# Gather issue, placement order and job pacing in a one-core graph layer

## The reference, cut to what matters

```
h = relu(layernorm(x))
feat = [h[src], h[dst]]                       # 8448 x 2048
e_f = relu(feat @ W_kind + b_kind)            # kind hh: edges 0..127, oo: next 640, ho: the rest
logit = e_f @ W_a + b_a
alpha = softmax of logit over the edges of one dst
z = segment_sum(alpha * h[src], dst)
h_new, o_new = relu([h, z] @ W_hn + b) on nodes 0..63, relu([h, z] @ W_on + b) on the other 192
x = x + [h_new, o_new]
h = relu(layernorm(x)); Wd = zeros.at[src, dst].add(edge_weight)
out = x + h @ Wd.T + bias
```

## Time and profile before

| | us |
|---|---|
| median of 3 runs (lowest, highest) | 346.76 (345.24, 348.99) |
| time of the profiled execution | 346.23 |
| its span on the core | 344.4 |

### The profile page before, as it was taken

How to read it: one execution, slowest core, us unless ns; L and a number is a source line. 1 busy time by engine, 2 the same in 40 slices (tenths; PEclk the granted TensorE clock), 3 DMA queues, 4 the chain that set the end, 5 groups by cost and what they waited for, 6 DMA issues and landing times.

```text
span 344.4 us, 4123 instructions
## 1 busy us (share of the span) xinstructions
PE 308.0 (89%) x1354; PEld 194.6 (57%) x1359; DVE 253.5 (74%) x428; ACT 177.0 (51%) x435; POOL 156.1 (45%) x148
## 2 busy tenths in 40 slices
PE   0899799999768999989999999999999786998992
PEld 0687488745425665556557576666653635543531
DVE  4655427369930699969969969978999799994334
ACT  3963342373441366654846657663638466564111
POOL 3210057237740277776757757774777610000000
PEclk9999899999989999999999999999999987899997
DMA  7999969969999789999999999999999999997003
GB/s 270 337 362 414 367 254 395 387 233 335 416 409 409 281 305 410 413 409 407 418 408 409 410 410 413 411 410 412 407 411 410 409 409 407 409 408 267 2 0 122
DMA packets 34425, 122.06 MB, mean 354 GB/s; under 512 B 4058, under 2 KB 4570, under 8 KB 34404
## 3 DMA queue, kind: packets, MB, share of 16 engines
q0 software_dynamic: 19008, 69.21, 51.3%
q1 hardware_dynamic: 14004, 47.34, 35.7%
q10 hardware_dynamic: 1392, 5.24, 3.8%
HBM read 115.49 MB, written 6.29 MB: 354 GB/s over the span
## 4 chain that ended last, share of the span: by engine, by line
PE 52%; DMA 18%; DVE 14%; ACT 4%; POOL 4%; issue 4%; another core or an unknown queue 3%; ACTq 0%; SPq 0%; DVEq 0%
PE psG L939 18%; DMA W<-weights 11%; PE psG L797 7%; DMA Gq<-q_ho,ids 6%; PE psG L908 6%; PE psW L847 5%; PE psA L847 5%; DVE Gp L637 4%; DVE Gp L633 3%; PE psB L847 3%; POOL Gq L353 2%; PE psG L1017 2%; POOL Gp L341 2%; DVE Wl L586 1%
## 5 line engine op out<-in xcount | busy, mean ns | idle before, releaser
L353 POOL DMA_INDIRECT Gq<-q_ho,ids x60 | 72.4, 1206 | 49.2 <-DVE Gp L633 21.9
L341 POOL DMA_INDIRECT Gp<-p_ho,ids x60 | 66.4, 1107 | 58.4 <-DMA p_ho<-T 27.7
L939 PE MATMUL psG<-W,hT 128*128 128x512 f32 x192 | 84.6, 592 | 0.0
L633 DVE TENSOR_TENSOR Gp<-Gp,Gq 128x1024 f32<-128x1024 f32 x65 | 79.2, 1219 | 2.7 <-DMA Gq<-q_ho,ids 2.7
L637 DVE SCALAR_TENSOR_TENSOR Gp<-Gp,wa 128x1024 f32<-128x1024 f32 x65 | 79.2, 1218 | 0.3
L448 ACT ACTIVATE RW<-ohs,ewh 128x256 fp32r<-128x256 f32 x66 | 33.3, 505 | 60.2 <-DVE ohs L624 31.4
L939 PEld LDWEIGHTS psG<-W,hT 128*128 128x128 f32 x192 | 35.5, 190 | 40.1 <-issue 40.1
L847 PE MATMUL psW<-RW,ohd 128*128 128x256 f32 x264 | 45.4, 294 | 2.5 <-ACT RW L448 1.2
L624 DVE TENSOR_SCALAR ohs<-iota,idf 128x256 fp32r<-128x256 f32 x72 | 26.6, 369 | 24.2 <-PE psA L847 13.3
L847 PEld LDWEIGHTS psW<-RW,ohd 128*128 128x128 f32 x264 | 36.9, 192 | 6.4 <-issue 4.1
L847 PE MATMUL psA<-RL,ohd 128*128 128x256 f32 x240 | 35.9, 295 | 3.4 <-ACT RL L458 2.8
(11 more groups left out here) (158 smaller groups left out, 348.8 us busy)
## 6 DMA issues: line engine op xcount, KB each, us to landing
W<-weights SPq DMA_DIRECT2D x67, 512.0 KB
Gp<-weights SPq DMA_DIRECT2D x8, 512.0 KB, 10.9
pre_f<-weights SPq DMA_DIRECT2D x3, 512.0 KB, 9.4
xs<-x SPq DMA_DIRECT2D x2, 512.0 KB, 4.0
h_rows<-h ACTq DMA_DIRECT2D x1, 1024.0 KB, 4.8
pre_l<-weights SPq DMA_DIRECT2D x2, 512.0 KB, 7.4
p_ho<-T ACTq DMA_DIRECT2D x2, 512.0 KB, 6.3
q_ho<-T ACTq DMA_DIRECT2D x2, 512.0 KB, 6.9
```

What stands on the lines that cost most here:

```text
L341: nc.gpsimd.indirect_dma_start(out=Gp[:, i % NP, :], out_offset=None, in_=p_oo if t <= OO_TILES else p_ho, in_offset=bass.IndirectOffsetOn ...
L353: nc.gpsimd.indirect_dma_start(out=Gq[:, i % NQ, :], out_offset=None, in_=q_oo if t <= OO_TILES else q_ho, in_offset=bass.IndirectOffsetOn ...
L633: nc.vector.tensor_tensor(Gp[:, i % NP, :], Gp[:, i % NP, :], Gq[:, i % NQ, :], ALU.add).then_inc(s_sum, 1)
L939: last = nc.tensor.matmul(psG[:, 2 * t + half, :], hT[:, k, t * P:(t + 1) * P], W[:, s, half * HALF:(half + 1) * HALF], start=u != 1 and k ...
```

## The change

The diff is short and stands here whole. (1) Gathers: before, p0 to p11 are issued in a row, then q0 to q7, then the rest as slots come free. After, p0 to p5 and q0 to q3 come first. The pairs (q4, p6), (q5, p7), (q6, p8), (q7, p9) wait for `s_wused` at 22, 24, 26 and 28, which is for chunks 5, 7, 9 and 11 of hh to be used; p10 and p11 wait for 30, chunk 13. The rest is as before. (2) Inside the hh unit the count of lot 0 comes after chunk 8 (was 9), that of lot 1 after chunk 10 (was 12), the place of lot 0 after chunk 11 (was 13). (3) `PACE`: the sum stays 30 over 20 lots, with two jobs left behind them; the first 24 jobs are spread over lots 3 to 17 instead of 3 to 15. Of the last eight jobs, 0, 1 and 2 go to lots 18, 19 and 20 (were 16, 17, 18), 3 and 4 both to lot 21 (were 20 and 21), 5 to lot 22 as before. (4) `BEFORE_OO` goes from 48 to 51: the oo lots are lots 18 and 19, `few_max` comes after lot 20 and `few_sums` after lot 21.

```diff
-BEFORE_OO = 48
+BEFORE_OO = 51
...
-PACE = [2, 2, 2, 2] + [2, 2, 1, 2, 1] + [2, 2, 2, 2] + [1, 1, 1, 0, 1, 1, 1]
+PACE = [2, 1, 2, 1, 2] * 3 + [1, 1, 1, 2, 1]
...
-            for i in range(NP):
+
+            for i in range(NQ - 2):
                 p_rows(i)
-            for i in range(NQ):
+            for i in range(NQ - 4):
                 q_rows(i)
+            for i in range(NQ - 4, NQ):
+                pool.wait_ge(s_wused, SPLIT + PRE + 1 + 2 * (i - NQ + 4))
+                q_rows(i)
+                p_rows(i + 2)
+            for i in range(NQ + 2, NP):
+                pool.wait_ge(s_wused, SPLIT + PRE + 9)
+                p_rows(i)
             for i in range(NQ, len(GATHERED)):
                 q_rows(i)
...
-                    elif i == 7:
+                    elif i == 6:
                         lot_count(0)
-                    elif i == 10:
+                    elif i == 8:
                         lot_count(1)
-                    elif i == 11:
+                    elif i == 9:
                         lot_place(0)
```

## The result

| | us |
|---|---|
| after, median of 4 runs (lowest, highest) | 352.30 (350.92, 353.16) |
| before, median of 4 runs (lowest, highest) | 346.00 (341.40, 348.99) |
| ratio after to before, 95% interval | 1.026 (1.015 to 1.037) |
| after, the profiled execution, and its span | 352.54, 350.7 |

Medians are over all executions, but every ratio leaves out slow ones, over 1.5% above the fastest of their kernel (346.76 and 348.99 here), so 1.026 stands for 352.3 against 343.3. How much the executions of the kernel before scatter differs from one chip to the next: 19 on the chip of e1 to e4 and 25 on that of e9 to e11 lay between 339.4 and 343.0 us, the 13 on the chip of e5 to e8 between 339.54 and 347.75, median 341.84. Against those 13 the changed kernel stood at 351.56, a ratio of 1.033 (1.026 to 1.041). The profile that the prediction was read from (346.23) was one of the longer ones.

What follows compares the result with a forecast made beforehand. Transfers at a 410 GB/s ceiling bound the kernel. 346.23 + 1.2 (gathers, placements) + 0 (pacing) + 0 (end) = 347.4, given as 347.5 us after 0.5 for the median; own range 344.5 to 350, with rivals 341.3 to 352.

Steps and rivals of the forecast that it cites:

- The ledger: Up to 130 us: bytes moved at the 410 GB/s ceiling decide the time; 29.0 MB before, 28.9 after, 0.2 us later.
- Rival (a): Up to 219 us: TensorE's progress sets the pace, the ledger is wrong; 341.5 us, chance 0.25.
- I take +1.2 us, near the low end, since weights are in flight at each release.: Gathers and placements, to 130 us: cost of transfers still in flight at 100.5 us when held gathers are released; +1.2 us.
- rival (c): At 80 to 100 us: thin releases open gaps of 2.2 us each, weights late in turn; 5 us, 352, chance 0.08.
- bounds to +9: Gathers and placements: up to 9 us later if each of four releases left an uncovered 2.2 us.
- +8 by it: Gathers and placements: the term if the fixed cost of about 2.0 us is read as a cost per release.
- a hole of 4 us: Kernel before, 118 to 130 us: transfers at 285 GB/s, costing 4 us, which the change would remove.
- the idle time at 57 to 80 us: Left by the held gathers, said to be paid back by the removed hole; 6 p rows worth 7.7 us of transfers.
- 31% for the weights: At 84 to 100 us: the weights' share while gathers are queued, read as 4.2 us for a chunk.
- The end, priced at 0: Last eight jobs: job 3 ends at 290 us, SyncE is out before the queue dries; 0, between -1 and +7.
- The 3.9 us credited to `few_max`: Near the end: `few_max` no longer stands between lot 20's tiles, moving job 3 forward by 3.9 us.
- rival (b): At the end: SyncE held by `load_top(5)` behind a later job while the queue is dry; 4 to 7 us, chance 0.13.

Runs made afterwards that it cites:

- e1: Kernel before with only the new gather order and its waits for chunks (part 1): 347.75 us against 340.79, ratio 1.019.
- e4: Kernel before with only the new pacing and the oo lots one lot later (parts 3 and 4): 342.85 us against 340.79, ratio 1.007.
- e9: Kernel before with p0 to p11 first as before and only q4 to q7 held for hh chunks: 344.57 us against 341.11, ratio 1.009.
- e11: Kernel before with p9 to p11 held until ScalarE has copied unit two, plus the sooner counts and places (part 2): 338.63 us against 341.11, ratio 0.994.
- e5: Kernel before, unchanged, for a second profile: median 341.84 us, profiled execution 341.35.
- e8: Kernel before with the oo lots one lot later and another pacing that keeps job 3 in lot 20: 343.88 us against 341.84, ratio 1.002.
- e10: Kernel before with p9 to p11 held until ScalarE has copied unit two: 338.51 us against 341.11, ratio 0.993.
- e6: The changed kernel, unchanged, again beside the kernel before on one chip: 351.56 us against 341.84, ratio 1.033.
- e7: Kernel before with the new gather order but without its waits for chunks: 351.64 us against 341.84, ratio 1.032.
- e12: Kernel before with p6 to p11 held until ScalarE has copied unit two: 351.26 us against 341.24, ratio 1.031.
- e3: Kernel before with the held gathers and the sooner counts and places (parts 1 and 2): 350.29 us against 340.79, ratio 1.028.
- e2: Kernel before with only the sooner counts and places of lots 0 and 1 (part 2): 341.10 us against 340.79, ratio 1.001.

## Why the prediction was wrong

**What held.** The ledger as a view: the rate ahead of 130 us goes with the time (14 points, 0.208 us for 1 GB/s against 0.205 worked out), and behind it all ran at 410 until 290. TensorE's steps in the hh unit: chunk 13 was used at 101.1 us (100.5 forecast) and hh was done at 104.5 (103.9). The logit of the hh tile begins where VectorE had waited for hh:
```profile
104.57 1.23 DVE L651 SCALAR_TENSOR_TENSOR psG<-psG,wa 128x1024 f32<-128x1024 f32 x1 [5.77 <-PE psG L916]
```
GpSimd's long wait and the hole went, no slice between 105 and 290 us fell under 400, and the low slices (148 to 240) stood at 61 to 88 us, forecast at 57 to 80 and 150 to 250. Rival (a) is dead: hh was done at 104.5 us where before it was done at 114.9, and that lead bought nothing.

**The step that failed: "I take +1.2 us, near the low end, since weights are in flight at each release."** The prediction had 16.8 MB moved by 100.5 us with one or two transfers in flight. Measured, 281 x 54.5 = 15.3 MB: 1.5 MB, three transfers, less. All of it went missing among the releases: up to 80 us 249 x 34 = 8.5 MB had moved, and the prediction's 16.8 MB less its 16 released transfers (8.4 MB) are 8.4. From 100.5 to 130 us it was as forecast (404 and 408 GB/s), but by then nothing could be regained. Between two releases only one pair of gathers and the one or two chunks for which slots are free are under way, and the rate was 179 GB/s from 80 to 84 us and 370 from 84 to 100.5. This is rival (c), which had a chance of 0.08 and a price of 5 us, by mechanism, though TensorE was never late with it; the term was +1.2 with bounds to +9, and measured against the execution that the prediction took as its base it is +4.3. The Trainium skill, page "DMA: Bandwidth & Descriptors", section "Anatomy of one DMA", puts about 2.0 us of fixed cost on each DMA of GpSimd's path. Read as a cost per release, the prediction had +8 by it; the measured 4.3 lies between the two, and for e9's four releases the 3.5 us are under half of what that reading would give.

**The base.** The prediction took the earlier trace rows for the kernel before as such: a hole of 4 us, chunks late by 10 us. e5 shows that they belong to an execution in which loads went out late. With the loads nearly on time the kernel before has nothing there to be regained, so the 4 us of hole that paid for the idle time at 57 to 80 us were no payment. Against e5 the idle time shows in full: 370 to 325 GB/s are 45 x 84 = 3.8 MB, 9.2 us, and the two profiled executions differ by 11.2. By stretches, 57 to 73 us lack 2.6 MB (212 GB/s for 376), 6.4 us, while six p rows stand behind q0, and 80 to 100.5 us lack 1.1 MB, 2.6 us, among the releases: next to an undisturbed kernel before, the rows moved behind q0 are the larger loss. The ratio of 1.033 against the larger sample of before, for 1.026 at first, fits with that. One execution with an unexplained wait in it was not a base for a ledger; the chain behind the earlier trace rows names that wait at 82.48 us, and the prediction leaves it out.

**The share of the queues.** The prediction read 31% for the weights as the chip's way to share, and held it against the Trainium skill. The same page of the Trainium skill, in its section "Queues, rings and completion order", has an engine take turns between its queues packet by packet. The share of both queues from 89 to 103 us in e5, where gathers were queued and the loads went out sooner:
```profile
q0 software_dynamic: 833, 3.03, 54.1%
q1 hardware_dynamic: 740, 2.70, 47.9%
```
About half each: by that rule, the trace agrees. (In e10, with no load late, it is 54.3% and 47.7%.) The 31% of the earlier trace rows was a queue with too few loads in it, since each went out about 4 us late. So in these rows gathers don't starve the weights, and the hold on them had nothing to protect.

**The end, priced at 0.** Job 3 ran from 289.8 to 293.7 us, where the prediction had 286.2 to 290, and `load_top(5)` was out with it. `few_max` had indeed gone out of lot 20's way, but the tiles came no sooner for that. VectorE and TensorE of the kernel after:
```profile
282.50 1.23 DVE L641 TENSOR_TENSOR Gp<-Gp,Gq 128x1024 f32<-128x1024 f32 x1 [1.27 <-DMA Gq<-q_ho,ids]
```
```profile
287.05 2.93 PE L855 MATMUL psA<-RL,ohd 128*128 128x256 f32 x12 [1.32 <-ACT RL L466]
```
The 3.9 us credited to `few_max` went at least in part into waits for q gathers, and the place of lot 20 took 2.93 us where the earlier trace rows have 1.41, at a granted clock of 0.50 from 287 to 290 us. The dip is 0.85 us in the kernel after, and 1.5 us in e4, where nothing ahead is late. This is rival (b) in small. A third part is not in the prediction: the last matmuls at the lower clock, 1.6 us; in e6 they take 3.64 us behind 3.62 idle, so it is no accident of one execution.

**The sum again**, against the profiled execution of before: 4.3 for the ledger, 0.4 more until the last load, 1.6 for the clock: 346.23 + 6.3 = 352.5, and 352.54 was measured. That it closes is no proof, since the terms are read from these two traces; what supports the first is e9, on another chip, with 3.5 us for four releases alone. Of the miss of 5.1 us, 3.1 are the mis-sized release term, 0.4 the end, 1.6 the clock.

**What stays open.** Why TensorE's increments come late. With the end of the matmul that frees a slot held against the issue of the load into it, loads are over 0.4 us late in before, e5, after, e6, e7, e8 and e12, up to 130 us by at most 4.9, 2.8, 2.4, 0.7, 13.5, 1.4 and 11.3 us; in the seven other profiles (e1 to e4, e9 to e11) none is over 0.2 us late from start to end. It goes with the chip or the series and not with the edit: e1 and e3, whose order and late rows are those of the changed kernel, have nothing of it, and the chips of e1 to e4 and e9 to e11 are those where the kernel before never took more than 343.0 us. In the seven disturbed profiles 4 to 12 of the 65 increments of `s_wused` are also missing from the record, in the others none. Whether recording has a part in the delay is not shown, and neither e7 nor e12 was repeated on a chip without it, so their 10 us each are not a price of their edits.

## What to carry to other kernels

Where the transfers are the ceiling, add up the bytes that are missing from it ahead of the point where they run full; hold back an issue only if other transfers cover the gap until the release, since several microseconds of nearly empty queues were not paid back here. Take the base of such a ledger from two profiled executions, and hold the issue of a late transfer against the end of the instruction that frees its slot before a hole is taken for the kernel's own. Where several microseconds vary from chip to chip, run a variant and its rival on one chip. The winner here filled the one thin stretch (three gathers kept for the wait on a store) and left the rest alone.

## What the hardware showed that was not expected

- Semaphore increments of TensorE that stand in the trace up to 13.5 us (e7) after the end of the matmul that makes them, several within 0.5 us (102.38 to 102.84 us in before), with each waiting load issued 0.01 to 0.02 us behind one, on two chips of four and in the first comparison. The kernel before took 346.2 us with four loads 3.9 to 4.9 us late in the hh unit and 341.4 with one 2.8 us late.
- A store of 1 MB in two parts: each lands 2.6 to 3.1 us behind its issue with six p gathers issued ahead (after, e1, e3, e6, e7), 3.3 to 4.2 with nine (e10, e11), and 5.6 to 8.0 with twelve (before, e2, e4, e5, e8, e9).
- 3.83 us of idle TensorE were followed by four matmuls in 3.61 us at a granted clock of 0.54; 1.11 us of idle time in the same place by the same four in 1.98 us at 1.00.
- One core sustains 410 to 411 GB/s over 90 us of gathers and loads mixed (130 to 220 us, all 14 profiles).
